# Flamingo block with four gated layers: the ReLU layer in three products of rounded parts, and weights of self attention loaded earlier

## What is computed

```
h1 = ln(x + mha(x, x, x, w1.., mask), g1, be1)          # self attention, 16 heads
h2 = ln(h1 + mha(h1, enc, enc, w2..), g2, be2)          # cross attention
ff = relu(h2 @ w_ff1 + b_ff1) @ w_ff2 + b_ff2           # 256 -> 1024 -> 256
out = ln(h2 + ff, g3, be3);  x = x + tanh(g) * out
```

## Time and profile before

| | |
|---|---|
| median of 3 runs | 2855.23 us (2855.07 to 2857.02) |
| profiled execution: its own time, its span | 2856.93 us, 2855.2 us |
| TensorE, VectorE, ScalarE, GpSimd busy | 89%, 62%, 47%, 39% of the span |
| mean granted TensorE clock | 0.943 of full |
| LoRA stage ends, query stage ends | 1207.9, 1252.9 us |
| ReLU stage | 1615.9 to 1734.4 us |

### The profile page before, as it was taken

One profiled execution on the slowest core, in us unless ns is written; L12 is line 12 of the kernel. 1 busy time (PEld: TensorE's weight loads), 2 busy tenths in 40 slices (PEclk: granted clock), 3 DMA queues, 4 the chain that ended last, 5 costly groups with the idle time before them and its releaser, 6 DMA issues.

```text
span 2855.2 us, 57262 instructions
## 1 busy us (share of the span) xinstructions
PE 2538.8 (89%) x21445; PEld 2082.6 (73%) x21445; DVE 1783.7 (62%) x3888; ACT 1342.7 (47%) x2700; POOL 1122.9 (39%) x1424
## 2 busy tenths in 40 slices
PE   7999799897997999889799899788868995999995
PEld 7999578794776777646477567656745875899995
DVE  5666588216874443278588446787778874666665
ACT  4444366324663111157566433444444563555563
POOL 3444411004113333347622233643453113777772
PEclk9999899998997999989999999889988996999998
DMA  8888776235660000063375300000018643565663
GB/s 226 241 245 242 217 197 171 101 122 142 192 186 16 1 1 1 18 167 90 94 203 155 120 0 6 1 1 1 1 30 221 174 119 134 202 222 208 202 224 112
DMA packets 145580, 357.06 MB, mean 125 GB/s; under 512 B 26064, under 2 KB 102480, under 8 KB 130816
## 3 DMA queue, kind: packets, MB, share of 16 engines
q1 hardware_dynamic: 133584, 268.38, 33.4%
q0 software_dynamic: 11760, 85.51, 8.4%
HBM read 260.55 MB, written 84.54 MB: 121 GB/s over the span
## 4 chain that ended last, share of the span: by engine, by line
PE 59%; DVE 11%; DMA 9%; POOL 6%; ACT 5%; issue 5%; SPq 3%; PEld 0%; POOLq 0%; PEldq 0%; ACTq 0%; DVEq 0%
PE ps L3259 8%; PE ps L1240 6%; PE ps L1250 5%; PE ps L1224 5%; DMA key_parts<-arena 5%; PE ps L3270 5%; PE ps L1836 3%; PE ps L724 2%; PE ps L2450 2%; PE ps L2159 2%; PE ps L2209 2%; POOL arena L428 2%; PE ps L939 2%; PE ps L2443 2%; PE ps L2199 2%
## 5 line engine op out<-in xcount | busy, mean ns | idle before, releaser
L1362 ACT ACTIVATE arena<-ps 125x448 f32<-125x448 f32 x768 | 404.6, 544 | 264.9 <-PE ps L1240 261.0
L1396 DVE TENSOR_REDUCE arena<-ps 112x2 f32<-112x750 f32 x384 | 348.0, 930 | 76.4 <-PE ps L1224 75.5
L502 POOL TENSOR_SCALAR ln_var<-ln_mv 112x1 f32<-112x1 f32 x160 | 43.0, 269 | 720.1 <-DVE ln_mv L496 715.5
L1240 PEld LDWEIGHTS ps<-arena,wreg 98*125 98x125 bf16 x2304 | 210.8, 140 | 68.2 <-issue 30.0
L3259 PE MATMUL ps<-moe_x_r,moe_w_r 128*128 128x256 f32 x2016 | 253.4, 287 | 5.6 <-DVE arena L3415 4.2
L3259 PEld LDWEIGHTS ps<-moe_x_r,moe_w_r 128*128 128x128 f32 x2016 | 247.3, 193 | 8.8 <-DVE arena L3415 3.8
L1240 PE MATMUL ps<-arena,wreg 98*125 98x112 bf16 x2304 | 233.2, 225 | 11.9 <-DMA arena<-values 3.7
L1224 PE MATMUL ps<-wreg,arena 96*112 96x375 bf16 x768 | 198.9, 345 | 20.8 <-DMA arena<-query_parts 6.0
L1250 PE MATMUL ps<-arena 125*17 125x112 f32 x6144 | 199.2, 263 | 0.6 <-ACT arena L1362 0.6
L428 POOL TENSOR_TENSOR arena<-arena 128x375 bf16<-128x375 f32 x128 | 114.3, 916 | 171.0 <-ACT arena L365 171.0
L285 PE MATMUL ps<-kv_ctx_r,kv_w_r 128*128 128x376 f32 x768 | 146.2, 339 | 22.1 <-DVE kv_w_r L391 14.5
(11 more groups left out here) (367 smaller groups left out, 5856.8 us busy)
## 6 DMA issues: line engine op xcount, KB each, us to landing
wreg<-key_parts SPq DMA_DIRECT2D x288, 187.5 KB, 3.8
key_parts<-arena SPq DMA_DIRECT2D x128, 281.2 KB, 4.1
values<-arena SPq DMA_DIRECT2D x64, 357.0 KB
arena<-values SPq DMA_DIRECT2D x64, 357.0 KB
arena<-query_parts SPq DMA_DIRECT2D x84, 224.0 KB, 4.4
arena<-key_parts SPq DMA_DIRECT2D x96, 187.5 KB, 4.0
wreg<-in_e_w SPq DMA_DIRECT2D x16, 704.0 KB, 5.4
query_parts<-arena SPq DMA_DIRECT2D x16, 672.0 KB, 5.6
```

What stands on the lines that cost most here:

```text
L1240: mm = pe.matmul(ps[0:KN, bank, g * T:(g + 1) * T], keys[r][:, hd, c * KN:(c + 1) * KN], queries(b)[:, hd, :], start=not masked, stop=not ...
L1362: act.activation(probs[k % PROBS], ps[0:KN, 4 + k % 2, 0:GT], ACT.Exp, scale=scale).then_inc(at_probs, 1)
L1396: dve.tensor_reduce(negmax[r % 2][:, 2 * p:2 * p + 2], ps[0:T, 2 * (p % 2):2 * (p % 2) + 2, 0:S2], AX.X, ALU.max, negate=True).then_inc(at ...
```

## The change

*ReLU stage.* Both weights are split into a high and a low part (`w1_r`, `w2_r`): high by ScalarE (w2 at the start of the stage, w1 behind group 0's ReLUs), low by GpSimd (w2 before, w1 behind the low parts of group 0's hidden tiles). The rows of groups 1 to 3 are split by VectorE (`split_rows`), those of group 1 behind the biases. Group 0's first products stay at full precision; those of the others are three products. All output products are three products. Group 0's hidden tiles are rounded by ScalarE, and their low parts made by GpSimd; in the other groups VectorE rounds all eight and makes the low parts of the even ones, GpSimd those of the odd ones. A batch's output products are ordered by parts: all eight of high by high, eight with w2's low part, eight with the hidden low parts; batch 0 of a group waits for each part as it comes. The full hidden tiles have one buffer instead of two. Semaphores of the LoRA stage are used again.

*Query stage.* w[0] and w[1] get a place at the front of `wreg` and are loaded by SP in the LoRA stage behind the last group's hidden products (`e1_hid`), where SP now waits until they are in. In the query stage SP loads the two rows, w[2] and w[3]; TensorE waits for no load, VectorE for these four. Keys and queries in `wreg` move up by 1024 words; two small arrays move to the arena.

The diff, cut to its core (left out: the new names of memory, a flag in the signature, one line of the return value):

```diff
@@ -651,15 +660,18 @@
                 self.now = [k for k in self.needed if k not in late]
-                self.rows = (1,) if kinds == 1 else (0, 1)
+                rows = tuple((attn_rows[:, r, :], lambda r=r: a["attn_rows"][self.s, r].partition_broadcast(128))
+                             for r in ((1,) if kinds == 1 else (0, 1)))
+                self.rows = () if late_rows else rows
+                self.late = rows[len(self.rows):] + self.late
                 self.ready = expect(len(self.now) + len(self.rows))
...
                     sp.dma_start(self.w[k], a["attn_w"][self.s, :, k]).then_inc(loaded, 16)
-                for r in self.rows:
-                    sp.dma_start(attn_rows[:, r, :], a["attn_rows"][self.s, r].partition_broadcast(128)).then_inc(loaded, 16)
+                for dst, src in self.rows:
+                    sp.dma_start(dst, src()).then_inc(loaded, 16)
@@ -788,11 +800,12 @@
                 wreg.clear()
+                wreg.take(128, 2, DC, D)
                 self.k = [wreg.take(SROWS, H, GT, dtype=BF16) for _ in range(2)]
                 self.q = [wreg.take(SROWS, H, GT, dtype=BF16)]
-                self.rows = wreg.take(128, DC, GT)
-                self.am = wreg.take(T, T)
                 self.pm = arena.place(KEPT_FREE_A, T, B, T)
+                self.rows = arena.place(KEPT_FREE_A + B * T, 128, DC, GT)
+                self.am = arena.place(KEPT_FREE_A + B * T + DC * GT, T, T)
                 self.masks_ready = expect(2)
@@ -829,19 +842,20 @@
-        def query_stage(s, kinds, dest, gate):
+        def query_stage(s, kinds, dest, gate, weights):
...
             parts = [arena.take(128, PARTS, DC * kinds, GT, dtype=BF16) for _ in range(G)]
-            q = Queries(s, kinds, parts, [arena.take(128, GT) for _ in range(G * DC * kinds)])
+            q = Queries(s, kinds, parts, [arena.take(128, GT) for _ in range(G * DC * kinds)], weights)
+            weights.expect_late()
             assert arena.at <= KEPT_FREE_A
...
             def sync(sp):
-                q.load(sp)
+                weights.load_late(sp)
                 q.spread_first(sp, 0, inputs.q[0], Q_PART, group_in[0])
@@ -855,12 +869,11 @@
-                dve.wait_ge(loaded, q.ready)
+                dve.wait_ge(loaded, weights.late_ready)
                 inputs.bias.scale(dve)
...
             def tensor(pe):
-                pe.wait_ge(loaded, q.ready)
                 q.project(pe)
@@ -2085,6 +2099,9 @@
                 sp.wait_ge(loaded, weights_ready)
+                sp.wait_ge(e1_hid, G * FC * 2)
+                following.load(sp)
+                sp.wait_ge(loaded, following.ready)
@@ -2409,8 +2427,14 @@
             arena.take(128, PK_HIGH_WORDS)
-            hid = [arena.take(128, FC, GT) for _ in range(2)]
+            arena.take(128, RELU_WORDS - PK_HIGH_WORDS)
             assert arena.at <= KEPT_FREE_A
+            w1_r = (relu_w1_high_r[:, :, :], relu_w1_low_r[:, :, :])
+            w2_r = (relu_w2_high_r[:, :, :], relu_w2_low_r[:, :, :])
+            hid_r = (relu_hid_r[:, 0], relu_hid_r[:, 1])
+            hid = arena.place(PK_HIGH_WORDS + FC * GT, 128, FC, GT)
+            PRODUCTS = ((0, 0), (0, 1), (1, 0))
+            POOL_LOW, DVE_LOW = (1, 3, 5, 7), (0, 2, 4, 6)
             added_bias = Bias(h, one[0:T, :], row[0:T, :])
@@ -2420,6 +2444,22 @@
             h0, out0, added0 = E * len(F0_ROWS), E * DC, B
+            ru_high, HIGH0 = e1_hid, G * FC * 2
+            ru_low_dve, LOW_DVE0 = e1_scaled, G * FC * 2
+            ru_low_pool, LOW_POOL0 = e1_act, G * FC * 2
+            ru_w_high, W_HIGH1 = e1_gate, G * FC * 2
+            ru_w_low, W_LOW1 = e1_both, G * FC
+            ru_x, X0 = e1_z, G * 2
+
+            def x_part(part, g):
+                return relu_x_high_r[:, :, :] if part == 0 else xn_t_r[:, :, g * GT:(g + 1) * GT]
+
+            def hid_low(eng, g, f):
+                eng.wait_ge(ru_high, HIGH0 + g * FC + f + 1)
+                return eng.tensor_tensor(hid_r[1][:, f, :], hid[:, f, :], hid_r[0][:, f, :].bitcast(F32), ALU.subtract)
+
+            def pool_lows(g):
+                return FC + (g - 1) * len(POOL_LOW) if g > 0 else 0
             SPLIT_AFTER, LOW_FROM = {1: (0,), 2: (1, 2)}, 8
@@ -2439,15 +2479,34 @@
                         pe.wait_ge(ffn_act, h0 + n - 1)
-                        for c in range(DC):
-                            mm = pe.matmul(ps[:, f % 2, 0:GT], w1[:, c, f * 128:(f + 1) * 128], xn_t[:, c, g * GT:(g + 1) * GT],
-                                           start=(c == 0), stop=(c == DC - 1))
+                        cols = slice(f * 128, (f + 1) * 128)
+                        if g == 0:
+                            for c in range(DC):
+                                mm = pe.matmul(ps[:, f % 2, 0:GT], w1[:, c, cols], xn_t[:, c, g * GT:(g + 1) * GT],
+                                               start=(c == 0), stop=(c == DC - 1))
+                        else:
+                            if f == 0:
+                                pe.wait_ge(ru_x, X0 + 2 * g)
+                                pe.wait_ge(ru_w_low, W_LOW1 + 2)
+                            for k, (wp, xp) in enumerate(PRODUCTS):
+                                for c in range(DC):
+                                    mm = pe.matmul(ps[:, f % 2, 0:GT], w1_r[wp][:, c, cols], x_part(xp, g)[:, c, :],
+                                                   start=(k == 0 and c == 0), stop=(k == len(PRODUCTS) - 1 and c == DC - 1))
                         mm.then_inc(ffn_h, 1)
-                    pe.wait_ge(ffn_act, h0 + (g + 1) * FC)
                     for q in range(GB):
                         pe.wait_ge(ffn_added, added0 + g * GB + q - 1)
-                        for f in range(FC):
-                            mm = pe.matmul(ps[0:T, 2 + q % 2, 0:D], hid[u][:, f, q * T:(q + 1) * T], w2[:, f, :], start=(f == 0), stop=(f == FC - 1))
+                        for k, (wp, hp) in enumerate(((0, 0), (1, 0), (0, 1))):
+                            if q == 0 and k == 1:
+                                pe.wait_ge(ru_w_low, W_LOW1 + 1)
+                            for f in range(FC):
+                                if q == 0 and hp == 0 and k == 0:
+                                    pe.wait_ge(ru_high, HIGH0 + g * FC + f + 1)
+                                elif q == 0 and hp == 1 and g > 0 and f in DVE_LOW:
+                                    pe.wait_ge(ru_low_dve, LOW_DVE0 + (g - 1) * len(DVE_LOW) + DVE_LOW.index(f) + 1)
+                                elif q == 0 and hp == 1:
+                                    pe.wait_ge(ru_low_pool, LOW_POOL0 + pool_lows(g) + (POOL_LOW.index(f) if g > 0 else f) + 1)
+                                mm = pe.matmul(ps[0:T, 2 + q % 2, 0:D], hid_r[hp][:, f, q * T:(q + 1) * T], w2_r[wp][:, f, :],
+                                               start=(k == 0 and f == 0), stop=(k == 2 and f == FC - 1))
                         mm.then_inc(ffn_out, 1)
@@ -2462,12 +2521,19 @@
                 act.wait_ge(early[0], weights.ready)
+                act.activation(w2_r[0], w2, ACT.Copy).then_inc(ru_w_high, 1)
                 def step(g, u):
-                    act.wait_ge(ffn_out, out0 + (g - 1) * GB)
+                    act.wait_ge(ffn_out, out0 + g * GB)
                     for f in range(FC):
-                        act.wait_ge(ffn_h, h0 + g * FC + f + 1)
-                        act.activation(hid[u][:, f, :], ps[:, f % 2, 0:GT], ACT.Relu, bias=b1[:, f:f + 1]).then_inc(ffn_act, 1)
+                        n = g * FC + f
+                        act.wait_ge(ffn_h, h0 + n + 1)
+                        act.activation(hid[:, f, :], ps[:, f % 2, 0:GT], ACT.Relu, bias=b1[:, f:f + 1]).then_inc(ffn_act, 1)
+                        if g == 0:
+                            act.wait_ge(ffn_act, h0 + n + 1)
+                            act.activation(hid_r[0][:, f, :], hid[:, f, :], ACT.Copy).then_inc(ru_high, 1)
+                    if g == 0:
+                        act.activation(w1_r[0], w1, ACT.Copy).then_inc(ru_w_high, 1)
@@ -2497,7 +2563,29 @@
+                def split_rows(g):
+                    dve.tensor_copy(x_part(0, g), xn_t[:, :, g * GT:(g + 1) * GT]).then_inc(ru_x, 1)
+                    dve.wait_ge(ru_x, X0 + 2 * g - 1)
+                    dve.tensor_tensor(x_part(1, g), xn_t[:, :, g * GT:(g + 1) * GT], x_part(0, g).bitcast(F32), ALU.subtract).then_inc(ru_x, 1)
+
+                def high(g, f):
+                    dve.wait_ge(ffn_act, h0 + g * FC + f + 1)
+                    dve.tensor_copy(hid_r[0][:, f, :], hid[:, f, :]).then_inc(ru_high, 1)
+
+                def split_hidden(g):
+                    for f in range(0, FC, 2):
+                        high(g, f)
+                        high(g, f + 1)
+                        hid_low(dve, g, f).then_inc(ru_low_dve, 1)
+
+                split_rows(1)
+
                 def step(g, u):
+                    if g > 0:
+                        split_hidden(g)
```

(39 more changed lines are left out.)

## The result

The changed kernel took **2852.06 us** in the median of 21 executions, against 2857.02 of the kernel before beside it (21 executions): a ratio of 0.9983 [0.9975, 0.9992], 4.9 us less. The forecast was 9.3 less (2846.0). The range of 2832 to 2854 held the time, but only because the rivals had stretched it: the forecast's own bounds end at 2850.5, and a gain of over 0.2%, which had a chance of 0.75, didn't come in this comparison. The three intervals have 5.2 to 7.1 us in common.

What follows compares the result with a forecast made beforehand. It took TensorE's products to bound the ReLU stage, and weight and row loads, then TensorE at its lower clock, the query stage's start; -5.6 and -3.7 made -9.3 us, a median of 2846.0, range 2832 to 2854.

Steps and rivals of the forecast that it cites:

- the forecast's own bounds: Whole kernel: 2841.5 to 2850.5 us from the bounds of the forecast's own terms, without the rivals.
- Query stage: Query stage: TensorE waits for no load, VectorE for the rows, tile 2 starts earlier; -5.6 us, bounds -7 and -3.
- Rival 4: Query stage: late rows hold VectorE as before, only TensorE starts early; -1 us there, 2850.6 in all; chance 0.08.
- Group 0: ReLU stage, first group: VectorE and GpSimd in one queue stall TensorE 9 us, then its clock is low; +7.8 us.
- rival 3: ReLU stage: TensorE's clock stays low until the end of group 1's first products; +6.8 us, 2862; chance 0.04.
- rival 1: ReLU stage: the VectorE-GpSimd lock hardly matters, no stall in group 0; -17 us there, 2832.6 in all; chance 0.12.
- Groups 1 and 2: ReLU stage, second and third groups: splitting work fits beside TensorE; a period of 22.4 us instead of 27.6.
- rival 2: ReLU stage: hand-overs of 0.2 us more per op make it -1 to +3 us; 2848.6 to 2852.6 in all; chance 0.14.
- Group 3: ReLU stage, last group: VectorE sets the end; batch 12 out at 1713.0, last addition at 1723.2 instead of 1726.9.
- ReLU stage: Whole ReLU stage: -3.7 us, bounds -18.6 and +3.
- Elsewhere all stages should keep their lengths: All stages other than query and ReLU: no change in length expected.
- the forecast's serial sum: ReLU stage: VectorE's and GpSimd's ops, roundings included, added one behind the other; in group 0 they end at 1641.6.

Runs made afterwards that it cites:

- Experiment 4: Changed kernel with VectorE's four bias additions at the ReLU stage's start cut from 2048 to 256 columns: 2846.27 us, 0.9939 of the kernel before; ReLU stage 105.9 us.
- experiment 5: Changed kernel with VectorE's first bias additions (to h) moved ahead of its wait for the rows: ReLU stage 114.5 us; one execution of 2862.31 us.
- Experiment 6: Changed kernel with ScalarE rounding the hidden tiles in all groups, VectorE making only low parts of the even ones: ReLU stage 113.4 us; one execution of 2870.08 us.
- experiment 7: Changed kernel with group 0's products needing no hidden low parts done first for all four batches: ReLU stage 113.6 us; one execution of 2869.03 us.

## Why the prediction was right, and where it was off

- **Query stage: -5.6 forecast, -5.3 measured** (45.8 to 46.5 in the ten profiled executions that have this part, 51.6 and 51.0 in two without it). The order of the waits was as told: TensorE at the barrier, then VectorE, tile 2 last. Only the load that VectorE waits for is another: the last of the four, a weight, and not the rows. The first remainder began at 1214.4 in the terms of before, not 1214.0; the four loads were issued over 2.3 us, not 1.2, and landed in 3.7, not 4.4. Rival 4 (remainder at 1218) is out.
- **Group 0: +7.8 forecast, +7.6 measured.** In the terms of before (7.35 less) the low parts ended at 1641.1 (forecast 1641.6) and the group at 1652.5 (1652.7). w2's subtraction took 4.53 (4.7), the stall 8.0 us (9), the window of 5.6 us behind it has the clock at 0.50 (rival 3, the clock low until 1660 and beyond, is out). One price was low: GpSimd's subtraction of 448 columns takes 1.09 to 1.15 us with VectorE out of the way, not 0.95. That the end still came within 0.5 us is in part luck: a turn of one addition and one subtraction took 3.15 where the sum has 3.20, so the additions cost less than their 2.25. Experiment 4 shows the cause: rival 1, the lock that hardly matters, is out. The Trainium skill (SBUF — State Buffer, the section on the two sides) has the lock held for a whole instruction; the 5.40 us of w2's subtraction in experiment 5 agree.
- **Groups 1 and 2: a period of 22.4 forecast, 22.5 measured.** So rival 2 (hand-overs eat the rest) is out. The time alone couldn't tell: 2852.06 lies within the 2848.6 to 2852.6 that rival 2 gives.
- **Group 3: the term that was mis-sized.** "Batch 12 is out at 1713.0": it was added at 1714.4. The last high part came when forecast (1710.9 for 1711.0), and the spacing of the additions behind it held (3.71, 3.70, 2.59), but the sum priced batch 12 at full clock. Behind the two waits the clock was at 0.50 for 3.2 us, which cost 1.2. This makes the last addition 1724.4 instead of 1723.2, and the **ReLU stage -2.4 instead of -3.7** (-2.4 to -3.5 in the four executions with this stage and no further edit). Experiment 6 takes away the waits, and the dip goes with them; experiment 7 keeps the waits and has no dip in group 3, so what decides it beside them stays open. In the six executions with the dip batch 12 came 0.8 to 1.5 us later behind the group's first product than in experiment 7. The forecast priced the lower clock behind the 9 us stall, and put it at nothing behind the 3 us hold.
- **The whole: -9.3 forecast; -7.8 by the stages, -4.9, -9.4 and -6.9 by the medians.** 1.2 of the 1.5 missing are group 3's dip. The rest of the distance to -4.9 stays open: -7.8 lies just outside that comparison's interval (2.3 to 7.1 us less), and the other two comparisons lie on both sides of it. "Elsewhere all stages should keep their lengths" can't be shown better than that scatter allows: the product-key stage took 390.3 and 390.5 with the ReLU stage of before and 390.5 to 393.2 with the new one (mean 391.9 of ten). A loss of about 1.5 us there is likely, and no run shows where it would come from.

## What to carry to other kernels

Before moving work to GpSimd because its busy share leaves room, list VectorE's large operations of the same stretch and add both up as one queue: it was this sum, not either engine's load, that gave the stall to within 1 us. When a step is found to be fed late, look for VectorE work that can go ahead of it, for a third engine that takes the small roundings, and for products whose inputs are there already: three edits of a few lines were worth about as much again (8 us) as the change itself. Price TensorE's waits with the lower clock behind them as a second value of the sum: two waits of 0.9 and 1.4 us cost 0.8 to 1.5 us more in six executions and nothing in a seventh.

## What was not expected of the hardware

- Two waits of TensorE of 0.90 and 1.40 us with two products between them were followed by 3 us at a granted clock of 0.50, in group 3 of the changed kernel, and two of 1.40 and 1.39 in group 1 of experiment 7 likewise. In experiment 6 a single wait of 0.51 at the place of group 3 was followed by none, and in group 3 of experiment 7 the same 0.90 and 1.40 weren't either.
- Behind the same stall of 8 us in group 0 the clock was low for 10.2 us in two executions of the changed kernel and for 6.8 in the third, both counted from its fall within the stall. The stage differed by 1 us with it.
- The scaling of 256 columns, 0.35 us alone, took 2.67 beside w2's subtraction, and two roundings of 448 columns 1.62 beside one of GpSimd's subtractions (0.69 for both when none ran): VectorE's scalings and roundings, with one input, wait as well, as the forecast's serial sum had them. Its additions of 256 columns with one input in PSUM took 0.39 to 0.42 us in the ReLU stage of every run.
- The changed kernel's 21 executions of the first comparison lie between 2844.96 and 2864.37 us. Its three profiled executions differed by 15 us (spans of 2850.5 and 2865.3), nearly all of it ahead of the LoRA stage, where the change puts nothing.
